# Local attention on one core: tiles of 64 queries against their 128 keys, and a score stage one tile ahead

## What is computed

```python
bk, bv = (look_around(bk), look_around(bv))      # window w-1 and w: 128 keys
sim = jnp.einsum('bhwid,bhwjd->bhwij', bq, bk)
mask = (i < j) | (i > j + WINDOW) | (j == -1)
sim = jnp.where(mask, -jnp.finfo(sim.dtype).max, sim)
attn = jax.nn.softmax(sim, axis=-1)
out = jnp.einsum('bhwij,bhwjd->bhwid', attn, bv)
...
x = x + o @ wo
```

## Time and profile before

| | us |
|---|---|
| median of 3 runs | 2807.44 |
| lowest and highest | 2797.06, 2808.77 |
| the profiled execution, its own time | 2814.0 |
| its span in the trace | 2812.3 |
| PE, DVE, ACT, POOL busy in the span | 2408.5, 1976.6, 1428.3, 379.6 |
| first `local_attend` (2287.7 to 2446.3) | 158.6 |
| second `local_attend` (2586.2 to 2745.9) | 159.7 |

### The profile page before, as it was taken

How to read it: one execution, slowest core, us unless ns; L and a number is a source line. 1 busy time by engine, 2 the same in 40 slices (tenths; PEclk the granted TensorE clock), 3 DMA queues, 4 the chain that set the end, 5 groups by cost and what they waited for, 6 DMA issues and landing times. The chain is left out here.

```text
span 2812.3 us, 40150 instructions
## 1 busy us (share of the span) xinstructions
PE 2408.5 (86%) x14416; PEld 1101.5 (39%) x14416; DVE 1976.6 (70%) x3999; ACT 1428.3 (51%) x2105; POOL 379.6 (13%) x559
## 2 busy tenths in 40 slices
PE   4799999999984499999959976999998789888997
PEld 2333333333322243333324433433333346534663
DVE  4789889888944588888735546888883765458553
ACT  1067677766772036777622221466775346533662
POOL 2000000000000100001100001000012243214330
PEclk8599999999997669999969985899997889988998
DMA  4300100000000510212200015012122333124320
GB/s 177 60 14 12 21 12 6 12 8 11 4 3 1 131 29 6 42 26 43 48 4 0 0 37 117 6 26 41 27 41 33 113 131 118 57 68 152 112 88 15
DMA packets 86068, 130.23 MB, mean 46 GB/s; under 512 B 28560, under 2 KB 50704, under 8 KB 83856
## 3 DMA queue, kind: packets, MB, share of 16 engines
q1 hardware_dynamic: 82592, 117.49, 16.9%
q10 hardware_dynamic: 3312, 10.59, 1.3%
HBM read 59.16 MB, written 13.63 MB: 26 GB/s over the span
## 5 line engine op out<-in xcount | busy, mean ns | idle before, releaser
L700 ACT ACTIVATE att_probs<-psum 128x1024 f32<-128x1024 f32 (+3 forms) x1152 | 1037.8, 951 | 628.9 <-PE psum L748 627.4
L658 DVE TENSOR_REDUCE att_part_max<-psum 128x1 f32<-128x512 f32 x1792 | 1128.1, 684 | 168.2 <-PE psum L730 164.3
L730 PE MATMUL psum<-k_rows,att_q_rows 64*128 64x512 f32 (+3 forms) x2304 | 822.7, 487 | 102.0 <-DMA att_q_rows<-q_pieces 55.3
L730 PEld LDWEIGHTS psum<-k_rows,att_q_rows 64*128 64x128 f32 x2304 | 363.1, 198 | 761.2 <-DVE att_part_max L658 535.2
L773 PE MATMUL psum<-att_probs,v_aug 128*9 128x512 f32 (+3 forms) x3712 | 450.4, 560 | 18.9 <-ACT att_z_sb L692 18.8
L748 PE MATMUL psum<-att_q_rows,k_rows 64*128 64x512 f32 (+3 forms) x2304 | 423.4, 409 | 14.0 <-ACT att_probs L700 9.7
L655 DVE CUSTOM_DVE_ANT_0 att_masked<-psum,mask_max_sb 128x384 bf16<-128x384 f32 (+3 forms) x512 | 232.9, 486 | 83.9 <-PE psum L730 79.1
L748 PEld LDWEIGHTS psum<-att_q_rows,k_rows 64*128 64x128 f32 x2304 | 242.5, 196 | 90.6 <-ACT att_probs L700 57.9
L608 POOL TENSOR_SCALAR_AFFINE_SELECT att_probs<-att_probs 128x256 f32<-128x256 f32 x256 | 102.5, 406 | 822.0 <-ACT att_probs L700 819.6
L1392 ACT ACTIVATE latt_probs<-psum,latt_bias,latt_scale 128x192 f32<-128x192 f32 x256 | 127.3, 507 | 120.3 <-DVE latt_bias L1431 120.3
L769 PE MATMUL psum<-att_probs,att_one_only 128*9 128x512 f32 (+3 forms) x1280 | 147.9, 534 | 10.7 <-ACT att_z_sb L692 10.5
(11 more groups left out here) (259 smaller groups left out, 2453.6 us busy)
## 6 DMA issues: line engine op xcount, KB each, us to landing
k_rows<-k_pieces SPq DMA_DIRECT2D x96, 256.0 KB, 8.0
lproj_swapped<-lproj_other SPq DMA_DIRECT2D x128, 128.0 KB, 2.1
latt_k<-local_k_T SPq DMA_DIRECT2D x32, 384.0 KB, 3.0
att_q_rows<-q_pieces SPq DMA_DIRECT2D x168, 64.0 KB
lproj_table<-in_tables SPq DMA_DIRECT2D x16, 512.0 KB, 4.2
latt_q<-local_q_T SPq DMA_DIRECT2D x32, 256.0 KB, 2.4
latt_v_own<-local_v_tok SPq DMA_DIRECT2D x32, 256.0 KB, 2.3
k_pieces<-proj_piece SPq DMA_DIRECT2D x24, 256.0 KB, 2.5
```

Source lines behind the costliest of these rows:

```text
L658: nc.vector.tensor_reduce(column, ring[e % NRING][:, 0:w], AX.X, ALU.max).then_inc(ring_free, 1)
L700: nc.scalar.activation(probs[s % NPROBS][:, pr, :, at:BANK], st[pr][:, :, at:BANK], ACT.Exp, scale=scale).then_inc(st_free, 1)
L730: nc.tensor.matmul(ring[e % NRING][:, 0:w], q_rows[u % NQ][rows, pr, qt * P:(qt + 1) * P].bitcast(F32R), k_rows[b][rows, pr, kc * BANK:kc ...
```

## The change

- A tile still holds two windows of queries, but each window of 64 queries is taken against its own 128 keys. A head's scores are two matmuls of 64 queries by 128 keys (one for each window w) that fill the upper and the lower half of a 128x128 result. A head has 128 columns of scores in place of 192. The mask comes first in the group, not last.
- The transposes are one 128x128 for each head, in two PSUM banks; `flip_past` and DVE's copy of it go.
- The outputs are matmuls of a window's 64 queries over its 128 keys. For that v is loaded so that partition p of `v_seen[:, w]` holds key p of the 128 that window w sees: for w = 1 the tile's own 128, for w = 0 the last 64 of the tile before and the first 64 of its own. The three transfers of v move 128, 256 and 128 KB.
- `scores(t, 0)` and `maxima(t, 0)` are moved one tile ahead: step i now holds scores and maxima of half 1 of tile i+1 and of half 0 of tile i+2. The order inside a step is written anew on each engine.
- `q_scale` comes by a transfer on SP's queue behind k, in place of DVE's copy.
- More steps stand written out ahead of and behind the loop (four and four, before two and two).

```diff
-            step(-1, 1, True, False, False)
-            step(0, 0, True, True, False)
-            with engine.Fori(0, NT // 2 - 1) as i:
-                step(2 * i + 1, 1, True, True, True)
-                step(2 * i + 2, 0, True, True, True)
-            step(NT - 1, 1, False, True, True)
-            step(NT, 0, False, False, True)
+            step(-1, 1, 0, 1, False, False)
+            step(0, 0, 1, 2, True, False)
+            step(1, 1, 2, 3, True, True)
+            step(2, 0, 3, 4, True, True)
+            with engine.Fori(1, NT // 2 - 2) as i:
+                step(2 * i + 1, 1, 2 * i + 2, 2 * i + 3, True, True)
+                step(2 * i + 2, 0, 2 * i + 3, 2 * i + 4, True, True)
+            step(NT - 3, 1, NT - 2, NT - 1, True, True)
+            step(NT - 2, 0, NT - 1, None, True, True)
+            step(NT - 1, 1, None, None, True, True)
+            step(NT, 0, None, None, False, True)
...
                 sp.dma_start(k[b][:, :, :], k_T[:, :, bass.ds(t * P, KEYS)]).then_inc(qk_in[b], 16)
+                after(sp, exp_done, (t - 1) * 2)
+                sp.dma_start(scale[b][:, :].unsqueeze(1), q_scale[:, bass.ds(t, 1), :]).then_inc(scale_in[b], 16)
 
             def values(t, b):
                 after(sp, o_full, t - 1)
-                past = v_tok[WINDOW:P, bass.ds(t, 1), :].rearrange("p t (m two d) -> p two (t m) d", two=2, d=LD)
-                for half in range(2):
-                    sp.dma_start(v_past[b][half * LD:(half + 1) * LD, :, :], past[:, half]).then_inc(v_in[b], 16)
-                sp.dma_start(v_own[b][:, :], v_tok[:, bass.ds(t + 1, 1), :].rearrange("p t d -> p (t d)")).then_inc(v_in[b], 16)
+                here, last = (v_tok[:, bass.ds(t + n, 1), :].rearrange("p t d -> p (t d)") for n in (1, 0))
+                sp.dma_start(v_seen[b][0:WINDOW, 0, :], last[WINDOW:P]).then_inc(v_in[b], 16)
+                sp.dma_start(v_seen[b][:, 1, :], here).then_inc(v_in[b], 16)
+                sp.dma_start(v_seen[b][WINDOW:P, 0, :], here[0:WINDOW]).then_inc(v_in[b], 16)
...
                 after(pe, exp_done, t * 2 + u - 1)
+                for half in range(2):
+                    nc.tensor.matmul(score[2 * half + u][:, 0:2 * P], ident_bf, bands[0 if first else 1], start=True, stop=False, skip_group_check=True)
                 for m in (2 * u, 2 * u + 1):
-                    even, odd = (score[2 * half + u][:, m % 2 * KEYS:(m % 2 + 1) * KEYS] for half in range(2))
-
-                    nc.tensor.matmul(even[:, 0:P], q[b][0:LD, m, :], k[b][0:LD, m, WINDOW:KEYS],
-                                     start=m % 2 == 0, stop=False, skip_group_check=True)
...
+                    for half in range(2):
+                        d = slice(half * LD, (half + 1) * LD)
+                        for w in range(2):
+                            queries = slice(w * WINDOW, (w + 1) * WINDOW)
+                            last = nc.tensor.matmul(score[2 * half + u][queries, m % 2 * P:(m % 2 + 1) * P], q[b][d, m, queries],
+                                             k[b][d, m, w * WINDOW:w * WINDOW + P], start=False, stop=True, skip_group_check=True)
                 last.then_inc(score_full, 1)
...
                 for m in range(NPAIR):
-                    for half in range(2):
-                        r = slice(half * LD, (half + 1) * LD)
-                        nc.tensor.matmul(o_ps[r, m * P:(m + 1) * P], v_own[b][:, (2 * m + half) * LD:(2 * m + half + 1) * LD], own_T[b][:, 2 * m + half, :],
-                                         start=True, stop=False, skip_group_check=True)
...
+                    for w in range(2):
+                        for half in range(2):
+                            at = m * P + w * WINDOW
+                            last = nc.tensor.matmul(o_ps[half * LD:(half + 1) * LD, at:at + WINDOW],
+                                                    v_seen[b][:, w, (2 * m + half) * LD:(2 * m + half + 1) * LD],
+                                                    probs_T[b][:, 2 * m + half, w * WINDOW:(w + 1) * WINDOW],
+                                                    start=True, stop=True, skip_group_check=True)
                 last.then_inc(o_full, 1)
...
-            def step(i, b, now, flip, put):
...
+            def step(i, b, t, ahead, flip_now, put):
+                if t is not None:
+                    scores(t, 1 - b, 1, isinstance(t, int) and t == 0)
+                if flip_now:
+                    flip(i, b, 0)
                 if put:
                     outputs(i - 1, 1 - b)
-                if flip:
-                    flip_own(i, b, 1)
-                if now:
-                    scores(i + 1, 1 - b, 1, first)
-                if flip:
-                    flip_past(i, b)
+                if flip_now:
+                    flip(i, b, 1)
+                if ahead is not None:
+                    scores(ahead, b, 0, False)
                 if put:
                     project_out(i - 1)
 
+            scores(0, 0, 0, True)
             steps(pe, step)
...
-            def step(i, b, now, flip, put):
-                if flip:
-                    own(i, b, 0)
-                if now:
-                    exponentials(i + 1, 1 - b, 0)
+            def step(i, b, t, ahead, flip_now, put):
+                if t is not None:
+                    exponentials(t, 1 - b, 0)
+                if flip_now:
+                    take_flipped(i, b, 0)
                 if put:
                     after(act, out_full, i - 1)
                     act.wait_ge(o_full, i)
                     nc.scalar.activation(o_T[:, :, :], o_ps.rearrange("p (m i) -> p m i", m=NPAIR), ACT.Copy).then_inc(o_done, 1)
-                if flip:
-                    own(i, b, 1)
-                if now:
-                    exponentials(i + 1, 1 - b, 1)
+                if t is not None:
+                    exponentials(t, 1 - b, 1)
+                if flip_now:
+                    take_flipped(i, b, 1)
```

More of the change, by code:

```diff
@@ L1316, in scores @@
-                    nc.tensor.matmul(odd, q[b][LD:P, m, :], k[b][LD:P, m, :],
-                                     start=m % 2 == 0, stop=False, skip_group_check=True)
-                    nc.tensor.matmul(even[:, P:KEYS], q[b][0:LD, m, :], k[b][0:LD, m, 0:WINDOW],
-                                     start=False, stop=False, skip_group_check=True)
-                for half in range(2):
-                    last = nc.tensor.matmul(score[2 * half + u][:, 0:2 * KEYS], ident_bf, bands[half][0 if first else 1],
-                                            start=False, stop=True, skip_group_check=True)
+                    for half in range(2):
[4 more added lines that the diff above has]
+                                             k[b][d, m, w * WINDOW:w * WINDOW + P], start=False, stop=True, skip_group_check=True)
@@ L1388, in exponentials, with take_flipped, step @@
                 if u == 0:
-                    after(act, past_full, t - 1)
+                    after(act, flip_full, t * 2 - 2)
                 for h in range(4 * u, 4 * u + 4):
                     m, half = divmod(h, 2)
-                    last = nc.scalar.activation(probs[b][:, h, :], score[2 * half + u][:, m % 2 * KEYS:(m % 2 + 1) * KEYS], ACT.Exp,
+                    last = nc.scalar.activation(probs[b][:, h, :], score[2 * half + u][:, m % 2 * P:(m % 2 + 1) * P], ACT.Exp,
                                                 scale=scale[b][:, h:h + 1], bias=bias[b][:, h:h + 1], accum_out=den[b][:, h:h + 1])
                 last.then_inc(exp_done, 1)
-            def own(t, b, u):
+            def take_flipped(t, b, u):
                 if u == 0:
                     after(act, o_full, t - 1)
-                act.wait_ge(own_full, t * 2 + u + 1)
-                nc.scalar.activation(own_T[b][:, heads_of(u), :], own_ps.rearrange("p (h i) -> p h i", h=4), ACT.Copy).then_inc(own_done, 1)
-            def step(i, b, now, flip, put):
-                if flip:
-                    own(i, b, 0)
-                if now:
-                    exponentials(i + 1, 1 - b, 0)
+                act.wait_ge(flip_full, t * 2 + u + 1)
+                nc.scalar.activation(probs_T[b][:, heads_of(u), :], flip_ps[u].rearrange("p (h i) -> p h i", h=4), ACT.Copy).then_inc(flip_done, 1)
+            def step(i, b, t, ahead, flip_now, put):
+                if t is not None:
+                    exponentials(t, 1 - b, 0)
+                if flip_now:
+                    take_flipped(i, b, 0)
                 if put:
@@ L1436, in inverses, with step @@
                 nc.vector.reciprocal(inv[b][:, heads_of(u)], den[b][:, heads_of(u)]).then_inc(inv_done, 1)
-            def step(i, b, now, flip, put):
-                if now:
-                    maxima(i + 1, 1 - b, 0)
-                    inverses(i + 1, 1 - b, 0)
-                    maxima(i + 1, 1 - b, 1)
-                if flip:
-                    after(dve, o_full, i - 1)
-                    dve.wait_ge(past_full, i + 1)
```

(13 more changed lines are left out.)

66 lines of the change are left out of this document (23 added, 43 removed).

## The result

| | before | after |
|---|---|---|
| median, us (4 runs each) | 2805.67 | 2693.03 |
| lowest and highest | 2797.06, 2808.77 | 2690.70, 2694.99 |
| profiled execution, its span | 2814.0, 2812.3 | 2694.99, 2693.1 |
| first `local_attend` (first q transfer to the end of the last addition) | 158.6 | 107.2 |
| second `local_attend` | 159.1 | 98.7 |

What follows compares the result with a forecast made beforehand. The prediction took a ring of ACT, DVE and POOL as the bound. Start 21, 13 tiles at 5.4 (70.2) and end 8.5 give 99.7 us a stage, 118 saved in all: 2690 us, range 2672 to 2732.

Steps and rivals of the forecast that it cites:

- ACT's ring: In both attention stages, a tile's 9.08 us is two successive turns of ACT, DVE and POOL; PE second at 8.48.
- Part 1: Half 0's scores and maxima ahead, scale by transfer: cuts the ring, removing 2.54 + 0.93 us idle; ACT, PE or transfers bound next.
- Part 2: ACT's work a tile: eight exponentials 3.5 us plus three copies of about 0.53 each, 5.1 us in sum.
- Part 3: PE's work a tile: scores 2 x 1.0, outputs 1.05, transposes 2 x 0.55, projection 1.09; 5.2 us, from 8.48.
- Part 4: SP's queue: k waits behind v, v for earlier outputs; this ring takes 10.5 us for two tiles, 5.25 each.
- handovers: Allowance where rings of 5.1, 5.2 and 5.25 us hand over to each other, giving 5.4 us a tile.
- p: Time a tile in us, forecast 5.4 (5.1 to 5.7); the median was to be 2549.4 + 26 p.
- Quarters one after the other: Rival on PE's scores: array quarters don't overlap fully, scores 1.45, PE 6.1 us a tile, 2708 us; chance 0.11.
- outputs slow: Rival on PE's output matmuls: they keep their pace, PE 7.1 us a tile, 2734 us; chance 0.08.
- maxima late: Rival on DVE's queue: maxima ahead held behind half 1's work, ACT idles, p = 6.4, 2716 us; chance 0.03.
- The lower clock for the whole stage: Rival: PE stays at 1.2 GHz, its 5.2 us becomes 10.0 a tile, 2821 us; chance 0.06.
- Late transfers: Rival on transfer landings: they come late, p = 6.0 to 6.3 us a tile, 2705 to 2713 us; chance 0.08.

Runs made afterwards that it cites:

- the version with nothing to wait for: Changed kernel with q and k issued ahead of v, scale last, and the outputs' copy out of PSUM moved from ACT to DVE: 2671.09 us.
- the repeat: The changed kernel itself, unaltered, run again on the same chip beside later runs: 2694.0 us, ratio 0.9586.
- the values cut short: Changed kernel with only 16 of 512 columns of each v transfer moved from the third tile on: 2687.12 us, ratio 0.9572.
- the keys ahead: Changed kernel with q and k of tile t+2 issued before v of tile t, scale last: 2685.1 us, ratio 0.9542.

## Why the prediction was right, and where it was off

**What bounded the kernel: right.** ACT's ring did, and PE stood close behind. Taking 0.8 us off PE's outputs moved nothing; taking the copy out of the ring moved the tile to PE's own sum. That sum was 8.22, not 8.48: the idle 0.60 was read as the whole price of the wait, which was 0.85.

**Part 1: right as a pair.** The cut ring was to leave three candidates, and it did. The copy held by POOL is shown by the same instruction at 1.40 and at 0.17 us. What the prediction didn't say is that, with the maxima ahead, the copy needn't be a transfer at all.

**Part 2, ACT, 5.1: measured 5.18.** Four exponentials take 1.74 us (forecast 1.76): in after from 2336.50 to 2338.24. The three copies have the rest, 0.57 each and not 0.53.

```profile
2336.50 0.45 ACT L1378 ACTIVATE latt_probs<-psum,latt_bias,latt_scale 128x128 f32<-128x128 f32 x1
...
2338.24 0.61 ACT L1386 ACTIVATE latt_probs_T<-psum 128x512 f32<-128x512 f32 x1
```

**Part 3, PE, 5.2: measured 4.98**, in the version with nothing to wait for. Scores 0.91 and not 1.0; outputs 1.09 against 1.05; transposes 0.58 and 0.49 against 0.55; projection 1.00 against 1.09, since the 1.09 was read behind a wait. So quarters of the array (row half and column half together) do work side by side, which no row of before showed: 16 matmuls of scores take 0.60 us, 0.037 each. The outputs' 32 come to 0.034 each, change of shape included. The Trainium skill (TensorE: Matmul & The Clock Gate, "Wait — 56ns, not 53.3ns?") has a floor of about 25 ns and a case of 62; both rates lie well under the 62, and nearer to the 25.

**Part 4, the transfers: the ring was right, the landings not.** v's first issue to k's issue is 2.74 (forecast 2.8), the landing 3.0, and the ring 10.55 for two tiles, where 10.5 was forecast. So the steady tile of the first stage is this ring, 5.28, and the 0.15 a tile added for handovers was 0.12 too much. In the second stage the steady tiles are 5.22 in the mean and PE's waits for k no more than 0.14, closer to ACT's 5.18. The load came out at 178 and 193 GB/s with shares of 0.57 and 0.62, against 200 and 0.6. The term that was mis-sized is the late landing. The prediction kept it to a rival with a price for every tile (6.0) at the worst landing seen, 4.5 us. It came otherwise: 3.0 in the loop, up to 5.4 us where the order enters and leaves the loop, in part after a late issue on SP's queue, and paid twice where PE's clock fell behind the gap. In the stage's sum, 20.1 + 78.4 + 8.7 = 107.2 and 19.4 + 70.6 + 8.7 = 98.7, the 13 tiles were forecast at 70.2: right for the second stage, 8.2 short for the first.

**The sum.** First projection at 21: measured 20.1 and 19.4. The end, 8.5: 8.7. The forecast's 118 was 6 too much by the stages; the median, 2693, is 3 above the 2690. That it came so near is in part luck. In the forecast's own terms p was 149.0/26 = 5.73 in the profiled execution, just beyond its 5.1 to 5.7, and 5.55 in the repeat. The late keys, which had a rival but no term, were partly paid for by the 0.15 a tile for handovers, which no row of before had asked for, and by a start that was 0.9 and 1.6 us shorter than forecast.

**The rivals.** Quarters one after the other, outputs slow and maxima late: each is ruled out by the rows above (0.92, 1.08, and L1378's few waits). The lower clock for the whole stage: no, 0.88 and 0.91; but for single tiles it was there, behind gaps, as in 2318.05 to 2321.51. Late transfers: in part, as told.

**What stays open.** Why k lands late just there. The traces hold the fetches of instructions too, 16 KB taking 0.9 to 1.7 us and 8 KB taking 0.3 to 0.6. Of the 352 transfers of k in the eleven traces, 25 took 4.0 us or more to land, and every one of them had such a fetch in flight within 3.0 us of its issue; of the 287 that had none, the slowest took 3.9. But 40 of the 65 with a fetch landed in under 4.0 us as well. The 1.30 us issue of the result's section, and its like in the repeat (1.04) and with the values cut short (1.14), also had a 16 KB fetch beside them. So fetches go with the late keys; that they cause them isn't shown, since no run moved them and they cluster, as the late keys do, around the stage's start and where the order enters and leaves the loop. v's bytes seem to lengthen the gap. With the keys ahead, a landing of 5.0 us is still there, and nobody waits for it.

## What to carry to other kernels

A wait and the work behind it must both go: of some 113 us, the order alone gave hardly more than the scale's transfer in it (25 and 19), the new tiles in the old order 78, and the last 35 came from the order once the tiles were small. Before an engine's sum is trusted as the next bound, take the whole stretch around its wait, from start to start, and not the idle that the page prints. When tiles get short, look at the transfers that stand behind others in one queue: put the one that is wanted first at the front, and give it slack for the slowest landing, since an idle TensorE may come back at half its clock.

## What the runs showed of the hardware

- Four quarters of 64 rows by 64 columns work side by side in fp32: 16 matmuls of 128 columns in 0.60 us, where 12 of the old ones (64 to 192 columns each), split by rows alone, took 1.03.
- A change between the shapes 128x64 and 64x64 costs 0.14 to 0.15 us each time: eight groups of four matmuls 0.37 us each, two groups of 16 1.02 each.
- A DVE instruction of a few numbers, a copy of 128x8 as well as a multiplication of 128x4, that starts while POOL is at its multiplication ends with it: the copy 1.40 beside 0.17 us (POOL at 128x768), the multiplication 0.42 beside 0.16 us (POOL at 128x512). Yet DVE's maxima, which read PSUM, took 0.75 and 0.76 us beside POOL and without it. The Trainium skill (SBUF — State Buffer, "SBUF: two separate sides") says which of DVE's instructions compete with GpSimd for a shared port pair, as an exclusive lock for a whole instruction: the fast forms of a copy, and those with two inputs in SBUF. The trace agrees: copy and multiplication are held, the maxima out of PSUM are not.
- The 384 KB transfer of k lands in 3.0 us in steady work, at a share of the transfer engines of 0.32 as well as of 0.6, and in up to 5.4 where the code enters or leaves the loop; with the share down at 0.37 to 0.40 it still came to 4.9 there. All 25 landings of 4.0 us or more had a fetch of instructions in flight beside them.
- Behind a gap of 2.63 us and one of 1.79 us TensorE worked at a granted clock of 0.50; behind gaps of 2.29, 1.85 and 1.70 it stayed at the upper level. So the length of the gap alone doesn't tell.
